# A GRU recurrence in a four-stage network: the gate inputs are copied into two small buffers by DMA, and waits are named in another order

## The reference

```python
def cell(h, x):
    gi = x @ W_ih + b_ih
    gh = h @ W_hh + b_hh
    i_r, i_z, i_n = jnp.split(gi, 3, axis=-1)
    h_r, h_z, h_n = jnp.split(gh, 3, axis=-1)
    r = jax.nn.sigmoid(i_r + h_r)
    z = jax.nn.sigmoid(i_z + h_z)
    n = jnp.tanh(i_n + r * h_n)
    h_new = (1.0 - z) * n + z * h
    return (h_new, h_new)
```

## Time and profile before

| what | value |
|---|---|
| median of 3 runs | 4613.4 us (4611.56 to 4613.57) |
| the profiled execution, its own time | 4612.59 us |
| its span in the profile | 4610.9 us |
| PE busy in the span | 3951.5 us (86%) |
| DVE, ACT, POOL busy | 2794.5 us (61%), 2078.2 us (45%), 517.3 us (11%) |
| first and last sum of ra on VectorE | 1233.8 us, 2846.2 us |
| granted TensorE clock over the span | 0.79 |

### The profile page before, as it was taken

One profiled execution on the slowest core, in us unless ns is written; L12 is line 12 of the kernel. 1 busy time (PEld: TensorE's weight loads), 2 busy tenths in 40 slices (PEclk: granted clock), 3 DMA queues, 4 the chain that ended last, 5 costly groups with the idle time before them and its releaser, 6 DMA issues. The chain is left out here.

```text
span 4610.9 us, 181370 instructions
## 1 busy us (share of the span) xinstructions
PE 3951.5 (86%) x69948; PEld 2957.6 (64%) x69948; DVE 2794.5 (61%) x11557; ACT 2078.2 (45%) x7520; POOL 517.3 (11%) x425
## 2 busy tenths in 40 slices
PE   1527686776999999999999998799789889988998
PEld 1424464453599999999999997366346435643663
DVE  7878787785666666666666665275247425722752
ACT  2016475576655555555555553153235314521542
POOL 3007356360000000000000000000100100010001
PEclk9999898998755555555555555899999989998999
DMA  2002132131000000000000002410221022012102
GB/s 82 0 24 89 33 103 74 42 103 55 0 0 0 0 0 0 0 0 0 0 0 0 0 0 75 196 45 14 88 114 41 37 105 73 28 73 110 46 14 82
DMA packets 77753, 201.33 MB, mean 44 GB/s; under 512 B 7290, under 2 KB 40058, under 8 KB 75136
## 3 DMA queue, kind: packets, MB, share of 16 engines
q1 hardware_dynamic: 77572, 198.94, 12.3%
HBM read 165.35 MB, written 33.57 MB: 43 GB/s over the span
## 5 line engine op out<-in xcount | busy, mean ns | idle before, releaser
L497 ACT ACTIVATE dit_prob<-dit_bank,dit_head_nbias 128x512 f32<-128x512 f32 x256 | 175.9, 687 | 351.0 <-DVE dit_head_nbias L515 350.6
L1390 DVE TENSOR_TENSOR_SCAN gru_state_parts<-gru_keep_gate,gru_new_and_old 128x24 f16<-128x24 f32 x1024 | 213.0, 208 | 174.1 <-ACT gru_new_and_old L1351 117.7
L1390 DVE TENSOR_TENSOR_SCAN gru_n_in<-gru_reset_gate,gru_candidate 128x24 f32<-128x24 f32 x1024 | 212.6, 208 | 82.3 <-ACT gru_reset_gate L1339 82.3
L1354 ACT ACTIVATE gru_hist<-gru_state 128x16 f32 x512 | 118.4, 231 | 310.8 <-DVE gru_state L1390 310.8
L1386 DVE TENSOR_REDUCE gru_r_in<-gru_sum_ra 128x8 f32<-128x16 f32 x512 | 89.5, 175 | 276.5 <-PE gru_sum_ra L1270 276.5
L1270 PE MATMUL gru_sum_za<-gru_state_parts,w_hh_hi 128*128 128x8 f16 x4096 | 254.6, 169 | 0.0
L1270 PE MATMUL gru_sum_na<-gru_state_parts,w_hh_hi 128*128 128x8 f16 x4096 | 254.6, 169 | 0.0
L1270 PE MATMUL gru_sum_ra<-gru_state_parts,w_hh_hi 128*128 128x8 f16 x4096 | 254.6, 169 | 0.0
L1260 PE MATMUL gru_sum_na<-gru_state_parts,w_hh_lo 128*128 128x4 f16 x4096 | 252.7, 166 | 0.0
L1260 PE MATMUL gru_sum_nb<-gru_state_parts,w_hh_lo 128*128 128x4 f16 x4096 | 252.1, 166 | 0.0
L1260 PE MATMUL gru_sum_ra<-gru_state_parts,w_hh_lo 128*128 128x4 f16 x4096 | 252.1, 166 | 0.0
(11 more groups left out here) (311 smaller groups left out, 13499.1 us busy)
## 6 DMA issues: line engine op xcount, KB each, us to landing
dit_w_qk<-w_qk_parts SPq DMA_DIRECT2D x64, 512.0 KB, 3.6
weights<-w_parts SPq DMA_DIRECT2D x8, 4096.0 KB, 12.2
weights<-w_out_parts SPq DMA_DIRECT2D x5, 4096.0 KB, 17.7
weights<-w_v_parts SPq DMA_DIRECT2D x5, 4096.0 KB, 12.2
small_given_w<-in_L_cond_qkv_w SPq DMA_DIRECT2D x48, 256.0 KB, 3.0
w_qk_parts<-small_parts_w SPq DMA_DIRECT2D x32, 256.0 KB, 2.1
small_given_w<-in_L_cond_ffn_w SPq DMA_DIRECT2D x32, 256.0 KB, 3.2
w_parts<-small_parts_w SPq DMA_DIRECT2D x32, 256.0 KB, 2.5
```

The costliest lines, as they stand in the source:

```text
L497: act.activation(self.prob[:, t % 2, :], self.S[t % 2], ACT.Exp, bias=bias[:, t:t + 1], scale=self.scale, accum_out=self.rsum[:, t:t + 1]) ...
L1354: act.activation(hist[:, :, :, at(i)].rearrange("p f b o -> p f (b o)"), state[:, 1 - par, :, :, LAST], ACT.Copy).then_inc(kept, 1)
L1390: return dve.tensor_tensor_scan(line(out), line(factor), line(term), 0.0, ALU.mult, ALU.add)
```

## The change

Two buffers `gi_now[0]` and `gi_now[1]` hold the gate inputs of two steps each. SyncE fills both at the start and then, in a loop of its own, refills each when TensorE has given it back (`now_taken`). TensorE's loop covers four steps, reads the buffers at addresses that don't depend on the index, waits for `now_loaded` at the first step of each buffer, and brings in the order zb, za, ra, rb. On VectorE and ScalarE only the order in which waits are named is changed, in several places; the first wait for `gn_ready` and for `r_a` is set off by one on both sides, which changes nothing.

```diff
+        NOW = 2
+        gi_now = [m.sb(f"gi_now_{v}", [P, NOW, 2, KD, 2, B], F16) for v in range(2)]
...
+            for v in range(2):
+                sp.dma_start(gi_now[v][:], gi_rz[:, v * NOW:(v + 1) * NOW]).then_inc(now_loaded[v], 16)
+            with sp.Fori(0, T // (2 * NOW) - 1) as n:
+                for v in range(2):
+                    sp.wait_ge(now_taken[v], n + 1)
+                    sp.dma_start(gi_now[v][:], gi_rz[:, at(n * (2 * NOW) + (2 + v) * NOW, NOW)])\
+                      .then_inc(now_loaded[v], 16)
...
-                          gi_rz[:, at(i), gate, fs[0]:fs[-1] + 1].rearrange("p o f e b -> p (o f e b)"),
+                                 gi_now[v][:, o, gate, fs[0]:fs[-1] + 1].rearrange("p f e b -> p (f e b)"),
...
-            with pe.Fori(0, T // 2) as pair:
-                for par in range(2):
-                    i = pair * 2 + par
+            with pe.Fori(0, T // (2 * NOW)) as n:
+                for s in range(2 * NOW):
+                    i, par, v, o = n * (2 * NOW) + s, s % 2, s // NOW, s % NOW
 
                     pe.wait_ge(z_in_b, i + 1)
-                    bring(zb_bank, Z_GATE, second, i)
+                    if o == 0:
+                        pe.wait_ge(now_loaded[v], n * 16 + 16)
+                    bring(zb_bank, Z_GATE, second, v, o)
+                    pe.wait_ge(z_in_a, i + 1)
+                    bring(za_bank, Z_GATE, first, v, o)
+                    pe.wait_ge(r_in_a, i + 1)
+                    bring(ra_bank, R_GATE, first, v, o)
                     pe.wait_ge(r_in_b, i + 1)
-                    bring(rb_bank, R_GATE, second, i)
-                    pe.wait_ge(z_in_a, i + 1)
-                    bring(za_bank, Z_GATE, first, i)
-                    pe.wait_ge(r_in_a, i + 1)
-                    bring(ra_bank, R_GATE, first, i)
+                    mm = bring(rb_bank, R_GATE, second, v, o)
+                    if o == NOW - 1:
+                        mm.then_inc(now_taken[v], 1)
...
+                    dve.wait_ge(r_a, i + 2)
                     dve.wait_ge(u_a, i + 2)
-                    dve.wait_ge(gn_ready, i + 1)
-                    dve.wait_ge(r_a, i + 1)
+                    dve.wait_ge(gn_ready, i + 2)
                     chain(n_in[:, A], reset[:, A], cand[:, par, A]).then_inc(n_in_a, 1)
...
+                    dve.wait_ge(n_a, i + 1)
                     dve.wait_ge(old_a, i + 1)
                     dve.wait_ge(keep_a, i + 1)
-                    dve.wait_ge(n_a, i + 1)
                     chain(new_parts[:, 0, A], keep[:, A], mix[:, A]).then_inc(hi_a, 1)
...
+                    dve.wait_ge(n_b, i + 1)
                     dve.wait_ge(old_b, i + 1)
                     dve.wait_ge(keep_b, i + 1)
-                    dve.wait_ge(n_b, i + 1)
                     chain(new_parts[:, 0, Z], keep[:, Z], mix[:, Z]).then_inc(hi_b, 1)
                     chain(new[:, Z], keep[:, Z], mix[:, Z]).then_inc(state_b, 1)
+                    dve.wait_ge(state_b, i + 2)
                     dve.wait_ge(hi_b, i + 2)
-                    dve.wait_ge(state_b, i + 2)
```

More of the change, by code:

```diff
@@ L1231, in gru_phase @@
         gn_ready, kept = m.sem("gn_ready"), m.sem("history_kept")
+        now_loaded = [m.sem(f"gi_now_loaded_{v}") for v in range(2)]
+        now_taken = [m.sem(f"gi_now_taken_{v}") for v in range(2)]
         back_turned, added, stored = m.sem("back_turned"), m.sem("added"), m.sem("gru_stored")
@@ L1248, in _, with bring @@
         def _(pe):
-            def bring(bank, gate, fs, i):
-                pe.matmul(bank[:, 0:HALF * 2 * B], scaled_ident[:],
-                          gi_rz[:, at(i), gate, fs[0]:fs[-1] + 1].rearrange("p o f e b -> p (o f e b)"),
-                          start=True, stop=False, skip_group_check=True)
+            def bring(bank, gate, fs, v, o):
+                return pe.matmul(bank[:, 0:HALF * 2 * B], scaled_ident[:],
+                                 gi_now[v][:, o, gate, fs[0]:fs[-1] + 1].rearrange("p f e b -> p (f e b)"),
+                                 start=True, stop=False, skip_group_check=True)
             def low(bank, gate, fs, ks, par, opens=False):
@@ L1351, in _ @@
                     act.activation(mix[:, Z, :, 0], n_in[:, Z, :, LAST], ACT.Tanh, scale=1.0 / GS).then_inc(n_b, 1)
+                    act.wait_ge(state_b, i + 2)
                     act.wait_ge(state_a, i + 2)
-                    act.wait_ge(state_b, i + 2)
                     act.activation(hist[:, :, :, at(i)].rearrange("p f b o -> p f (b o)"),
@@ L1379, in _ @@
             dve.engine_nop().then_inc(made, 1)
-            for s in (r_in_a, r_in_b, z_in_a, z_in_b, u_a, u_b):
+            for s in (r_in_a, r_in_b, z_in_a, z_in_b, u_a, u_b, r_a, gn_ready):
                 dve.sem_inc(s, 1)
@@ L1423, in _ @@
                     dve.tensor_tensor(mix[:, Z, :, LAST], z[:, Z], old[:, Z, :, LAST], ALU.mult).then_inc(old_b, 1)
+                    dve.wait_ge(state_a, i + 2)
                     dve.wait_ge(hi_a, i + 2)
-                    dve.wait_ge(state_a, i + 2)
                     dve.tensor_tensor(new_parts[:, 1, A, :, LAST], new[:, A, :, LAST], new_parts[:, 0, A, :, LAST],
                                       ALU.subtract).then_inc(lo_a, 1)
+                    dve.wait_ge(n_b, i + 1)
                     dve.wait_ge(old_b, i + 1)
                     dve.wait_ge(keep_b, i + 1)
-                    dve.wait_ge(n_b, i + 1)
                     chain(new_parts[:, 0, Z], keep[:, Z], mix[:, Z]).then_inc(hi_b, 1)
                     chain(new[:, Z], keep[:, Z], mix[:, Z]).then_inc(state_b, 1)
+                    dve.wait_ge(state_b, i + 2)
                     dve.wait_ge(hi_b, i + 2)
-                    dve.wait_ge(state_b, i + 2)
                     dve.tensor_tensor(new_parts[:, 1, Z, :, LAST], new[:, Z, :, LAST], new_parts[:, 0, Z, :, LAST],
```

## The result

The changed kernel takes 4445.32 us (median of 4 runs, 4443.65 to 4447.41) where the kernel before takes 4613.48 (4 runs, 4611.56 to 4616.73): the ratio is 0.9635, 95% interval 0.9618 to 0.9652, so 168 us or 3.6% faster. The forecast of 4462 was 17 us too high, and the time lies in its range. The profiled execution took 4447.41 us, with a span of 4445.7.

A forecast was written before the change was run, and what follows sets the result against it. TensorE's step, with slow brings, was taken as the bound, the VectorE and ScalarE chain 0.2 us behind. 512 × (3.155 − 2.86) = 151 us off the profiled 4612.59, with 0.8 added for the median, gave 4462 us; range 4425 to 4530.

The forecast's parts named there:

- What bounds the kernel: TensorE's recurrence step of 3.155 us, four brings taking 0.49; the VectorE and ScalarE chain has 0.2 us of slack.
- (1) Fixed addresses: TensorE's brings: no register instructions in most steps, 0.11 us in place of 0.49, TensorE's own step about 2.73 us.
- (2) Waits named in another order: VectorE's waits on the chain: 0.10 us won before `hi_a`, 0.03 before `n_in`; step 2.84 us, taken as 2.86.
- The rival that reordering does nothing: VectorE's 0.13 us gaps belong to ScalarE signals as such; step 2.97 us, time 4518 us; chance 13%.
- The term that was mis-sized: Gap from sigmoid to `n_in` on VectorE: only 0.03 us won, because `u_a` then sits on the separate wait instruction.
- the boundary that it added: TensorE's loop boundary, slower to its first bring: 0.02 us a step added for what does not hide.
- the rival of the deeper gain: `u_a` doesn't hinder `n_in`; `rb`'s place in VectorE's queue sets 2.82 us, 4442 us, down to 4396; chance 12%.
- The queue bound of 2.82 us: `hi_a` stands 0.13 us behind the sum of `rb` in VectorE's queue, so a step takes no less than 2.82 us.
- (3) Half Z: Second half of the features: `hi_b` and `lo_b` both keep more than 0.1 us before TensorE's waits, reordered waits as cover.
- (4) The copies: SyncE's 32 KB copy every second step: wanted after 8.5 us, landing takes 1.8 to 2.1; nothing shows.
- (5) The loop body: TensorE's loop of four steps, some 400 products, estimated at 51 KB: taken to stay on the chip without new fetches.
- The fetch rival: TensorE's four-step body does not stay: 127 branches at 3.3 us, 419 us more, 4881 us; chance 10%.

## Why the prediction was right

**What bounds the kernel** is confirmed from both sides: reordering alone gives nothing, because the brings hold `na` (3.150 us), and the copies alone give half (2.994 us), because the chain then holds it. In the prediction's words the chain had "0.2 us of slack"; the copies alone could use 0.161 of it. In the median step `hi_a` ended 0.24 us ahead of `na` before and ends 0.06 ahead in the kernel with the copies alone; of these 0.18 TensorE's restart (below) takes 0.02 back.

**(1) Fixed addresses.** As predicted: brings 0.03 us apart, all ahead of `na`. That TensorE alone would take 2.73 us a step was not run. The longer loop is worth at most 0.007 a step alone.

**(2) Waits named in another order.** The rival that reordering does nothing foresaw 4518 us; without the reordering the kernel takes 4530.7, with it 4445.3. `hi_a` gained its 0.10 (0.096 a step when it is undone). The term that was mis-sized is `n_in`'s, of which the prediction says "I count 0.03 there, not 0.10". The gap after the sigmoid shrank from 0.13 to 0.06 in the median step, and undoing it costs 0.071. The step behind it was to charge `u_a`'s signal, on the separate wait instruction, with the 0.13 that ScalarE's signals took on that path. Measured, `n_in` starts 0.09 after the sum of `na` ends (2001.52 + 0.18 = 2001.70 to 2001.79), and `lo_b` in the old order 0.11 after `state_b` ends: both signals are VectorE's own. That `u_a` still held `n_in`, as the prediction said, is shown by the kernel with `na` first.

In numbers: the forecast of 2.86 less 0.05 for `n_in`, less 0.02 for a loop boundary that costs nothing, plus 0.02 for TensorE's first four products after a wait (2002.54 to 2002.67, where four took 0.11 in the kernel before) and 0.01 for a ScalarE instruction of 0.22, is 2.82. That the forecast came within 17 us is in part luck: the boundary that it added and the restart that it left out cancel. The time therefore came out where the rival of the deeper gain had it (4442, 12%), though by a mechanism between the two: `u_a` and, 0.01 us behind it, the sum of rb in VectorE's queue both hold `hi_a`. The queue bound of 2.82 us was right to 0.01: with `u_a` out of the way the step stops at 2.813. That too is partly luck, since in this bound the sum of rb stands 0.13 ahead of `hi_a`, where 0.11 was measured, and the restart of 0.02 is missing.

**(3) Half Z.** "The reordered waits matter here as cover" is shown: with the old order there alone, 48 of the 168 us are lost. The prediction had `hi_b` end 0.18 and `lo_b` 0.20 us ahead of their products; measured it is 0.14 and 0.16, and less than 0.06 can't be, the signal's way. The 15 us later expected for the old order there had the slack right (0.13 and 0.15) and failed on what can be spent of it: it left out the signal's 0.06 and TensorE's restarts.

**(4) The copies** cost 0.001 us a step, and land in 1.7 us of the 8.5 allowed.

**(5) The loop body.** The body of four steps stays: no packet after the first pass, in the change and with the loop alone. The fetch rival was right in kind: a body twice as long is fetched and turns 3.6% faster into 2% slower. Its price was too low, 3.3 us a pass against 8 to 9.5. By the 256 instructions that the Trainium skill gives to a line of 16 KB ("Advanced Engine Details and Errata", ISA Cache) the bodies of two, four, eight and sixteen steps are, as an estimate, 26, 51, 101 and 203 KB. Its "Only 2 cache lines!" (32 KB) would have had the second fetched anew in each pass; the trace disagrees. Its 128 KB for TensorE agrees with three of the four loops; the third, under 128 KB by itself, is fetched in every second pass, in 9 packets, which at 16 KB each are 144 KB. That what is fetched ahead must find room too, and makes it too large, would fit; no run here shows it.

## What to carry to other kernels

Where an engine's stream and a chain through other engines end close together, price an edit on one by the slack of the other: here 0.005 and 0.16 us a step alone became 0.33 together. Name the signal that comes last first, also on chains that are not the bound yet, and put what need not wait for the chain ahead of the wait: one product of 0.03 us behind it cost 13 us over 512 steps. Before a loop is unrolled further, look at its branch's longest time and at the instruction queue's packets; a median hides a fetch in every second pass.

## What the runs showed of the hardware

- With a dynamic address, and the register instruction that works it out, four brings stand 0.12 us apart; at fixed addresses 0.03.
- A signal that the waiting instruction carries costs 0.03 us on VectorE, from ScalarE (2002.25 to 2002.28) as from VectorE itself (`state_b` ends at 2003.49, `lo_b` starts at 2003.52). One on a separate wait instruction costs 0.12 to 0.13 from ScalarE, and 0.09 to 0.11 from VectorE's own last instruction.
- On TensorE a loop body of four steps (some 800 instructions) stays for 127 passes; one of eight (some 1600) is fetched in every second pass, one of sixteen in every pass. A fetched pass costs 8 to 9.5 us, of which the branch shows 4 to 5.
- After a wait TensorE's first four products take 0.13 us to the next, instead of 0.11.
